# Cross-attention: background weight fetches tied to the rows of maxima, their sums moved within six groups

## What is computed

```python
x = _layernorm(x + _L0_attn_ref(x, ...))
x = _layernorm(x + _L0_xattn_ref(x, ctx_512, ctx_512))   # the stage of the change
x = _layernorm(x + _L0_ffn_ref(x, w_gate, w_up, w_down)) # its weights are prepared in it
...
def _L0_xattn_ref(q, k, v):      # 32 query heads of 16, 8 key heads, no projections
    scores = jnp.einsum('bkgsd,bktd->bkgst', qh, kh) / scale
    weights = jax.nn.softmax(scores, axis=-1)
    out = jnp.einsum('bkgst,bktd->bkgsd', weights, vh)

def weight_quant(w):             # for each of the three feed-forward weights
    scale = 1.0 / jnp.clip(jnp.mean(jnp.abs(w)), EPS)
    wq = jnp.clip(jnp.round(w * scale), -1.0, 1.0) / scale
```

## Time and profile before

| what | value |
|---|---|
| median of 3 runs | 3013.24 us (3006.34 to 3014.74) |
| the profiled execution | 3024.37 us, of which its span is 3022.6 us |
| busy in the span | PE 71%, DVE 62%, ACT 39%, POOL 24% |
| cross-attention, first score pair to last exponential | about 548 to 1048 us of the span |
| in 530 to 1060 us, DVE's maxima (line 875) | 309.4 us busy, 256 of 1224 ns |
| in 530 to 1060 us, ACT's exponentials (line 824) | 279.8 us busy, 512 of 598 ns |
| POOL's cutting of a chunk | 5455 + 5439 + 4087 ns (lines 771, 772, 776) |

### The profile page before, as it was taken

One profiled execution on the slowest core, in us unless ns is written; L12 is line 12 of the kernel. 1 busy time (PEld: TensorE's weight loads), 2 busy tenths in 40 slices (PEclk: granted clock), 3 DMA queues, 4 the chain that ended last, 5 costly groups with the idle time before them and its releaser, 6 DMA issues. The chain is left out here.

```text
span 3022.6 us, 34926 instructions
## 1 busy us (share of the span) xinstructions
PE 2150.8 (71%) x12276; PEld 1443.4 (48%) x12308; DVE 1864.1 (62%) x3042; ACT 1173.5 (39%) x2024; POOL 734.7 (24%) x584
## 2 busy tenths in 40 slices
PE   5999993777778748888848999983002768777770
PEld 5777772222222224554527777761001647555550
DVE  3555663767777546666554555555887343588876
ACT  2322321675555613333322322223784111365540
POOL 1112122045865100000001112220000040466644
PEclk7999996798887879999968999997555579999995
DMA  4332323552532020000013323310000200599965
GB/s 132 92 64 64 64 43 120 146 164 69 159 107 68 11 98 0 0 0 0 0 63 71 63 56 64 64 22 16 0 0 0 100 1 0 205 306 303 306 213 167
DMA packets 83528, 258.63 MB, mean 86 GB/s; under 512 B 17312, under 2 KB 18592, under 8 KB 73168
## 3 DMA queue, kind: packets, MB, share of 16 engines
q0 software_dynamic: 29856, 153.33, 17.0%
q1 hardware_dynamic: 52528, 103.41, 12.4%
q10 hardware_dynamic: 1024, 0.26, 0.0%
HBM read 168.30 MB, written 37.79 MB: 68 GB/s over the span
## 5 line engine op out<-in xcount | busy, mean ns | idle before, releaser
L875 DVE TENSOR_REDUCE x_negm<-x_M 128x2 f32<-128x1024 f32 x256 | 309.4, 1224 | 114.5 <-PE x_M L935 113.9
L824 ACT ACTIVATE x_PT<-x_T 128x512 f32<-128x512 f32 x512 | 279.8, 598 | 205.1 <-PE x_T L955 200.2
L317 ACT ACTIVATE L_attn_PT<-L_attn_T 128x512 f32<-128x512 f32 x320 | 175.6, 595 | 360.3 <-PE L_attn_T L519 360.1
L387 DVE TENSOR_REDUCE L_attn_negm<-L_attn_M 128x2 f32<-128x1024 f32 (+1 forms) x192 | 192.1, 1041 | 57.7 <-PE L_attn_M L500 57.3
L955 PE MATMUL x_T<-x_QS,x_KS 49*128 49x512 f32 x512 | 142.9, 555 | 64.7 <-ACT x_PT L824 44.4
L224 POOL DMA_DIRECT2D L_attn_QKS<-L_attn_HL x64 | 35.0, 546 | 596.8 <-ACT L_attn_HL L302 563.0
L517 PE MATMUL L_attn_T<-L_attn_QKS 97*128 97x256 f32 (+3 forms) x512 | 165.8, 385 | 10.4 <-DMA L_attn_QKS<-L_attn_mT 8.4
L1380 PE MATMUL graph_P<-ident,graph_L 128*128 128x128 f32 x64 | 15.7, 427 | 219.8 <-DVE graph_L L1453 214.5
L964 PE MATMUL x_O<-x_PT,x_V 128*32 128x512 f32 x1024 | 157.3, 691 | 8.0 <-issue 8.0
L1401 ACT ACTIVATE graph_seen_a<-graph_SIM,graph_mid 128x512 bf16<-128x512 f32 x200 | 141.4, 708 | 40.4 <-DVE graph_mid L1433 40.4
L955 PEld LDWEIGHTS x_T<-x_QS,x_KS 49*128 49x128 f32 x512 | 52.8, 203 | 216.2 <-ACT x_PT L824 134.0
(11 more groups left out here) (369 smaller groups left out, 5859.6 us busy)
## 6 DMA issues: line engine op xcount, KB each, us to landing
L_attn_QKS<-L_attn_HL SPq DMA_DIRECT2D x192, 128.0 KB, 4.7
L_attn_QKS<-L_attn_HL POOLq DMA_DIRECT2D x192, 128.0 KB, 4.1
moe_y_rows<-slots_YS SPq DMA_DIRECT2D x48, 256.0 KB, 7.6
x_WRAW<-in_w_gateT POOLq DMA_DIRECT2D x8, 1024.0 KB, 7.4
x_QS<-x_xh SPq DMA_DIRECT2D x128, 64.0 KB, 2.4
x_WRAW<-in_w_upT POOLq DMA_DIRECT2D x8, 1024.0 KB, 5.3
x_WRAW<-in_w_downT POOLq DMA_DIRECT2D x8, 1024.0 KB, 5.9
ffn_w<-x_WTER POOLq DMA_DIRECT2D x12, 512.0 KB, 3.5
```

The costliest lines, as they stand in the source:

```text
L317: ac.activation(PT[:, s, bank], T[:, bank], ACT.Exp, scale=SCALE).then_inc(t_free, 1)
L387: last = ve.tensor_reduce(negm[:, g % 2, h0:h0 + nh, i], src, AX.X, ALU.max, negate=True)
L824: ac.activation(PT[:, s // 4, head(s), :], T[(STEPS_S * g + s) % 3][:], ACT.Exp, scale=SCALE).then_inc(t_free, 1)
L875: ve.tensor_reduce(negm[:, g % 2, u // 4:4:2, u % 4], m[:].rearrange("p (r k) -> p r k", r=2), AX.X, ALU.max, negate=True).then_inc(m_free, 1)
```

## The change

It has three parts, all in the background work.

1. **When chunks are fetched.** `fetch(c)` now first waits, on POOL, for the row of group `FETCH_GROUP[c]`: two fetches in each of groups 0, 1, 2, 3, 4 and 7, then one in each of groups 8 to 12, 15 to 20 and 23. The first two fetches are thereby also moved from the start of the stage to the row of group 0.
2. **When they are summed.** The 24 pieces go from groups 0 to 5 (after s = 2, 6, 10, 14) to groups 0 to 4 and 7 (after s = 8, 10, 12, 14).
3. **POOL's order.** In `cut_weights` the next fetch stands behind the chunk's last DMA instead of ahead of the subtraction. The residual additions and norms stand apart: addition 0, chunks 0-1, norm 0, chunks 2-5, addition 1, chunks 6-7, norm 1, chunks 8-11, addition 2, norm 2.

```diff
+        SUM_GROUPS = (0, 1, 2, 3, 4, 7)
+        FETCH_GROUP = [g for g in SUM_GROUPS for _ in range(2)] + [8, 9, 10, 11, 12, 15, 16, 17, 18, 19, 20, 23]
...
             def fetch(c):
+                pool.wait_ge(shifted, 32 * (FETCH_GROUP[c] + 1))
...
             def sum_weights():
-                fetch(0)
-                fetch(1)
-                for c in range(12):
-                    pool.wait_ge(sized, 2 * c + 2)
-                    fetch(c + 2)
+                for c in range(14):
+                    if c >= 2:
+                        pool.wait_ge(sized, 2 * (c - 2) + 2)
+                    fetch(c)
...
                     pool.wait_ge(compared, 2 * c + 2)
-                    if c + 2 < 12:
-                        fetch(c + 14)
                     gp.tensor_tensor(ter, below, ter, ALU.subtract).then_inc(ter_made, 1)
...
                     pool.dma_start(FW["scratch"][w][:, q, :], ter).then_inc(ter_out[c % 2], 16)
+                    if c + 2 < 12:
+                        fetch(c + 14)
...
             sum_weights()
-            for b in range(NB - 1):
-                cut_weights((range(0, 2), range(2, 7), range(7, 12))[b])
...
+            add_residual(0)
+            cut_weights(range(0, 2))
+            apply_norm(0)
+            cut_weights(range(2, 6))
+            add_residual(1)
+            cut_weights(range(6, 8))
+            apply_norm(1)
+            cut_weights(range(8, 12))
+            add_residual(2)
+            apply_norm(2)
...
-                    if g < 6 and s % 4 == 2:
-                        piece = 4 * g + s // 4
+                    if g in SUM_GROUPS and s in (8, 10, 12, 14):
+                        piece = 4 * SUM_GROUPS.index(g) + (s - 8) // 2
```

More of the change, by code:

```diff
@@ L744, in fold, with add_residual, apply_norm @@
                 pool.wait_ge(folded, folds)
-            def sum_weights():
-                fetch(0)
-                fetch(1)
-                for c in range(12):
-                    pool.wait_ge(sized, 2 * c + 2)
-                    fetch(c + 2)
+            def add_residual(b):
+                pool.wait_ge(m_free, drained("turn", KV * b + KV - 1))
+                gp.tensor_tensor(Z[b % 2][:], Z[b % 2][:], X[:, b, :, :], ALU.add).then_inc(added, 1)
+            def apply_norm(b):
+                pool.wait_ge(moments, MOMENTS * (b + 1))
+                for i in range(NT):
+                    gp.tensor_scalar(X[:, b, i, :], Z[b % 2][:, i, :], ln["mean"][:, i:i + 1], ln["rstd"][:, i:i + 1],
+                                     ALU.subtract, ALU.mult).then_inc(applied, 1)
+            def sum_weights():
+                for c in range(14):
+                    if c >= 2:
+                        pool.wait_ge(sized, 2 * (c - 2) + 2)
+                    fetch(c)
                 fold(wpart[:].rearrange("p q w -> p w q"), 8)
```

## The result

| what | before | after |
|---|---|---|
| median | 3013.99 us (4 runs) | 3062.07 us (4 runs, 3060.25 to 3071.23) |
| ratio | | 1.0171, interval 1.0144 to 1.0198 |
| the profiled execution, its span | 3024.37, 3022.6 us | 3060.25, 3058.5 us |
| cross-attention, first score pair to last exponential | 500.2 us | 552.7 us |
| from the stage's first transfer on SP to the first score pair | 50.0 us | 44.8 us |

A forecast was written before the change was run, and what follows sets the result against it. PE, DVE and ACT hand tiles around in fixed order, so group time was taken as the bound. Terms -4.8 + 8 - 6.5 - 2.6 + 8.3 + 8.8 + 4.5 = +15.7 on the median 3013.24 gave 3029 us, range 3008 to 3042.

The forecast's parts named there:

- Addition 0: Group 9: batch 0's residual addition comes late, DVE stands 13.5 us instead of 5.17; +8.3 us, bounds +5 and +13.
- Addition 1: Group 17: DVE stands 7.3 us instead of 0.99 for batch 1's residual, +6.3; lost clock in group 18, +2.5.
- Addition 2: Group 25: DVE stands 1.4 or 6.3 us, depending on group 23's clock; with lost clock +4.5, bounds +1 and +9.
- Start: Stage opening: fetches 0 and 1 no longer run beside the unload of x; -4.8 us, bounds 0 and -6.
- Group 5: Unload group: three fetches leave, SP's own backlog stays; 21.4 to 16 us, -5.3, plus -1.2 in group 6.
- Groups 20 to 23: Fetch 22 lands in the unload of x, so one collision replaces another; -0.8 us.
- Group 13: Fetch 16 lands in the unload of x, one collision replacing another; -1.8 us, bounds with group 21 -7 and +5.
- the first rival: Rows come back whole: fetches alone delayed rows 6, 14, 22, so groups 5, 13, 21 gain; 3014 us, chance 0.20.
- The pieces: Groups 0 to 4 and 7: four pieces in the second half lengthen ACT's work; +8 us, bounds +4 and +14.
- The rival of the clock falling in the summing groups: Low clock takes five groups from 15.2 towards 16.3 us and lengthens stalls; +7 more, 3036 us, chance 0.10.
- The rival of the late chunks: Fetched chunks land late, ACT waits at s = 8, 2 to 4 us in each of six groups; 3047 us, chance 0.08.
- The rival of the ties: Where POOL is later, `FETCH_GROUP` changes no time; groups 13 and 21 get 3 us longer each; 3036 us, chance 0.07.

The follow-up runs named there:

- e3: Changed kernel with POOL reordered so it cuts nothing under the moments of batches 0 and 2, still two chunks under batch 1's: 3033.25 us, ratio 1.0071.
- e1: Kernel before with only POOL's new order of additions, chunks and norms; fetches and pieces unchanged: 3035.41 us, ratio 1.0082.
- e9: Kernel before with fetches, pieces and addition 0 moved, POOL idle under all moments, chunks dealt 5, 4, 3 behind the norms: 3007.91 us, ratio 0.9902.
- e10: Kernel before with only POOL's order changed: chunks dealt 1, 5, 4, 2 around the additions, POOL idle under moments: 3027.26 us, ratio 0.9972.
- e8: Changed kernel with POOL's comparisons and subtraction of chunks 0 and 1 replaced by memsets of like length: 3063.57 us, one execution.
- e4: Changed kernel with each of POOL's cutting instructions split in four of 128x512, same order: 3055.80 us, ratio 1.0137 to the kernel before.
- e5: Changed kernel without the waits for rows from fetch 2 on: 3082.05 us, ratio 1.0144 to the kernel before.

## Why the prediction was right and wrong

The direction was right, and the reason I gave for it, late additions, was a real one, but by e3 it is less than a third of what groups 9 and 10 lost (7.6 of 25.1 us).

**The step that failed** is a term put at nothing, in the sentence that the writes, the fetches "and the norms' new places cost nothing: POOL has idle time there and nobody waits". POOL's idle time there was not free. It stood still exactly while DVE did the moments, and the chunks that fill it block these steps; for cutting under the moments the sum has no term at all. It measured 17.5 us in groups 9 and 10 by e3; in groups 17 to 19 the excess over the forecast is 17.9, at a blocked time of 20.3, and e1 has 16.9 there without any wait for an addition. e1 shows the order alone at +0.8%. The profile before held the hint: POOL waited up to 33.2 us for the moments, and every moment step took 0.14 to 0.17 us. I had read the wait as slack. Rows in which the two engines never run together say nothing of what happens when they do, and I should have bounded it from both sides instead of taking zero.

A bound stood in the same profile, in the last stage, whose rows the prediction does not use. There DVE takes a difference of two tensors in SBUF (L1990, 48 times) beside one of POOL's, and needs 2.90 us in the median where the shortest took 1.22:

```profile
2632.20 2.40 POOL L1862 TENSOR_TENSOR slots_WL<-slots_RAW,slots_WH 128x1024 fp32r<-128x1024 f32 x1
2632.76 2.93 DVE L1990 TENSOR_TENSOR slots_WL<-slots_RAW,slots_WH 128x1024 fp32r<-128x1024 f32 x1
...
2936.70 1.22 DVE L1990 TENSOR_TENSOR slots_WL<-slots_RAW,slots_WH 128x1024 fp32r<-128x1024 f32 x1
```

POOL's instruction ends at 2634.60, and DVE's ends 1.09 us after that, about its own length: it had stood for most of POOL's. (The last sentence of that paragraph of the prediction named norm 0 or 1 holding DVE's next moments, which did not happen.)

**Addition 0**: right in kind, small in size. 13.5 us of standing was forecast, 16.1 measured; from fetch 13 at 684.27 to the addition at 700.12 it was 15.8 us, where 13.7 was taken (12.1 in group 9 and 1.6 ahead of it). The cost to the groups, 7.6 us by e3, is near the +8.3: with a longer stall than forecast, that nearness is partly luck.

**Addition 1**: 7.3 forecast, 4.75 measured; but the blocked batch 0 ahead of it had moved everything, so the term cannot be read alone. **Addition 2**: 6.67 us, where I had 1.4 to 6.3 and chose between; groups 25 and 26 cost +7.7 instead of +4.5, since group 23 ran at full clock.

**Start**: right. The second half of x takes from 510.97 to SP's first keys at 515.98, 5.0 us instead of 9.9. **Group 5**: right, 15.9 us where 16 was forecast; group 6, however, gained nothing (16.5, was 15.1), so the term was -4.1 and not -6.5. The timelines of SP and PE in after, against the earlier trace rows:

```profile
637.53 1.33 SPq L690 DMA_DIRECT2D x_QS<-x_mT  x2
```

```profile
625.20 0.51 PE L969 MATMUL x_T<-x_QS,x_KS 49*128 49x512 f32 x2
...
641.10 0.50 PE L969 MATMUL x_T<-x_QS,x_KS 49*128 49x512 f32 x2 [2.54 <-DMA x_QS<-x_mT]
```

SP issues the row at the same moment as before (637.53 against 637.78) and it lands 4.9 us sooner: the backlog stays and the share of the DMA engines comes back, as the sum took it. Group 6, which both the sum and the rival of the rows coming back whole wanted faster, still had four of its eight pairs at 0.79 or 0.80 us, the low clock.

**Groups 20 to 23**: -12.5 instead of -0.8, the largest miss beside the lock. I had fetch 22 some 16 us into group 20, in the unload of x. It was issued at 922.10, 7.6 us into the group, and landed 6.7 us later; SP's unload began at 931.44, and fetch 23 was held for the row of group 23. No fetch ran beside the unload, and groups 21 to 23 took 15.1, 13.1 and 13.1. **Group 13** is the other half of that term: PE no longer waits for row 14 either, so what the first rival had as its sign, neither row 14 nor row 22 keeping PE waiting, came true. But group 13 ran whole at the low clock (0.50 from 779.90 to 799.56) and took 19.7 us instead of 18.9. So the first rival's gain came at one place beside the -5.5 of group 5 that it shares with the sum, and it was eaten by the lock; without that gain the change would have come out still slower. That groups 13 and 21 fall to 16 was named as a sign of being wrong: 21 did, 13 did not.

**The pieces**: +9.9 instead of +8. Groups 2 and 3 took 17.0 us, not 15.2; group 1, which kept the full clock, 14.7 and group 7 14.0. The rival of the clock falling in the summing groups, given 0.10, was thus half true: three low stretches of 6.8 us, in groups 2, 3 and 4. The rival of the late chunks failed: ACT waited for no chunk. The rival of the ties failed too: fetch 22 had landed before the unload, and group 21 did not get longer.

The rest adds up: groups 9, 10 and 17 to 19, the two places of the lock, make 34.7 us over their forecast, where the whole was missed by 31.6; pieces, group 6, addition 2 and group 13 make another 9, while groups 20 to 23 gave 11.7 back. What the clock alone cost was not tried: how much of the 17.5 us is standing and how much is the low clock behind it stays open.

## What to carry to other kernels

Before you fill one engine's idle time, look at who works in it: an engine that is idle because it waits for another may be the reason why that other runs at full speed, and small VectorE steps on SBUF next to long GpSimd instructions are the case to look for. Compare the mean durations of the lines that the change does not touch, before and after; here a mean of 159 ns that became 2940 pointed at the cause at once. And treat a background engine's order as a budget between the foreground's deadlines: the version that pays, e9, leaves POOL idle through every batch's moments and deals its chunks so that no addition is late. These two alone, in the kernel before, were worth 0.3% (e10); with them e9 has the fetches moved, at the start, in group 5 (15.0 us instead of 21.4) and in group 21 (16.6 instead of 20.0). Which of these makes the rest of its 1.0% was not tried apart.

## What the hardware showed unexpectedly

- A TENSOR_SCALAR step of VectorE on 128x4 numbers in SBUF lasts until GpSimd's running instruction ends: 0.17 us became 5.38 in group 10 and 6.05 in group 18 (int32), and 0.17 became 5.91 in e8 (f32, L76, beside a comparison). The size of GpSimd's instruction sets the length: in e4 no step took over 1.18 us, and that one (L72) stood under subtractions of 1.15. A large step pays the wait on top of its own work: 2.93 us instead of 1.22 for L1990 in the profile of before.
- The kinds differ. Steps with two tensors from SBUF are let go before the end of GpSimd's comparison: L66 ended at 713.76, 1.7 us before L784, and L70 at 724.89, 1.7 us before L783; under the subtraction they stood to its end (L75 to 736.17, L786 to 736.15). Under memsets they are not held at all, and TENSOR_SCALAR steps still are. Neither the maxima from PSUM nor the BATCH_NORM_STATS2 steps (at most 0.70 us each, many of them beside a GpSimd instruction) were held in any run.
- The longest step began ahead of the instruction that held it: L72 at 870.61, while POOL issued a fetch (870.35 to 871.13), lasted until the comparison behind that issue ended at 876.63. L70 at 720.70 began in the same way. Whether the issue itself holds a step stays open: with nothing but an issue beside it, a step took 0.16 us in e8 (L72, 853.79) and another 0.40 in e5 (L76, 870.71), to within 0.02 us of the issue's end.
- GpSimd pays nothing visible for it: its comparison took 5.43 to 5.46 us with and without blocked steps beside it. It can be the one that waits: in the last stage of before its L1862 step at 2925.04, begun 0.23 us behind VectorE's L1990, took 3.23 us instead of 2.41. That is one case.
- Standing still is not the only way to a low clock: at 842 to 908 us PE was 72% busy in stops and starts, and its granted clock stayed at 0.51 for the whole stretch.
